# Conv stream of a fused metaformer kernel: two passes of 108 rows with shifts made by four loads a step, in place of three passes of 72 rows and one load

## The reference

```
z = layernorm over channels (x)
z[:, :12] = conv3x3(z[:, :12], w_pc)          # 12 -> 12 channels, zero padding
z = 1x1 conv to 254 channels
z = irfft2( rfft2(8x8 patches of z) * fft_w ) # per channel frequency weights
a, b = halves of z;  x = x + 1x1 conv to 48 ( gelu(a) * b )
t = x as tokens; x = t + FFN( layernorm(t) )  # FFN rounds operands to fp8 (5,2), sums to (5,10)
```

## Time and profile before

| | |
|---|---|
| median of 3 runs | 765.3 us (762.51 to 765.31) |
| profiled execution | 768.14 us, its span 766.3 us, mean granted TensorE clock 0.976 |
| PE busy | 696.4 us (91%) |
| DVE, ACT, POOL busy | 579.6, 550.7, 475.1 us |
| DMA | 62.22 MB, 46492 packets, mean 81 GB/s |
| conv stream on PE (L501) | 384 matmuls, 29.5 us busy |
| taps load (L413) | 32 loads of 292.5 KB |

### The profile page before, as it was taken

One profiled execution on the slowest core, in us unless ns is written; L12 is line 12 of the kernel. 1 busy time (PEld: TensorE's weight loads), 2 busy tenths in 40 slices (PEclk: granted clock), 3 DMA queues, 4 the chain that ended last, 5 costly groups with the idle time before them and its releaser, 6 DMA issues.

```text
span 766.3 us, 18085 instructions
## 1 busy us (share of the span) xinstructions
PE 696.4 (91%) x5547; PEld 507.1 (66%) x5547; DVE 579.6 (76%) x1092; ACT 550.7 (72%) x1090; POOL 475.1 (62%) x356
## 2 busy tenths in 40 slices
PE   1249999999999999999999999999999999999952
PEld 1138777767777777677677776677777777767720
DVE  4614888888888888868888888888888888877651
ACT  3133477778777887767788777878788887766774
POOL 2544666666776676657666766667766776643342
PEclk9998999999999999999999999999999999999985
DMA  3342332333333433234334323333323332231001
GB/s 71 74 91 69 81 73 75 81 99 99 101 74 92 98 98 81 75 93 100 71 94 95 94 67 88 95 100 100 100 66 98 95 98 78 60 98 43 22 21 41
DMA packets 46492, 62.22 MB, mean 81 GB/s; under 512 B 19039, under 2 KB 34871, under 8 KB 46391
## 3 DMA queue, kind: packets, MB, share of 16 engines
q1 hardware_dynamic: 46151, 60.94, 31.9%
q10 hardware_dynamic: 240, 0.05, 0.1%
HBM read 44.62 MB, written 16.35 MB: 80 GB/s over the span
## 4 chain that ended last, share of the span: by engine, by line
PE 73%; DVE 10%; issue 7%; ACT 4%; DMA 2%; POOL 2%; SPq 1%; ACTq 1%; DVEq 0%; POOLq 0%
PE inva L468 15%; PE invb L473 15%; PE mixp L457 12%; PE misc L569 8%; PE misc L528 5%; DVE gmix L845 4%; PE misc L501 4%; PE misc L554 3%; PE misc L627 3%; ACT y L733 3%; PE misc L510 3%; PE misc L482 2%; PE misc L585 2%; DVE st L922 2%; DVE tch L869 1%
## 5 line engine op out<-in xcount | busy, mean ns | idle before, releaser
L845 DVE TENSOR_TENSOR gmix<-mixp,freq_w 128x508 f32<-128x508 f32 x256 | 163.3, 679 | 41.5 <-PE mixp L457 41.5
L457 PE MATMUL mixp<-win,zc 60*128 60x254 f32 x1024 | 145.7, 403 | 6.0 <-DVE gmix L845 2.2
L672 ACT ACTIVATE hid<-misc 128x512 f16<-128x512 f32 x192 | 100.9, 599 | 56.3 <-PE misc L528 56.3
L468 PE MATMUL inva<-inv,gmix 128*127 128x128 f32 x1024 | 136.1, 276 | 1.1 <-DVE gmix L845 1.1
L473 PE MATMUL invb<-inv,gmix 128*127 128x128 f32 x1024 | 135.2, 275 | 0.0
L468 PEld LDWEIGHTS inva<-inv,gmix 128*127 128x127 f32 x1024 | 130.1, 193 | 5.3 <-issue 3.7
L1033 POOL TENSOR_TENSOR tcen<-tpix,st 128x768 f32<-128x768 f32 x32 | 47.2, 1476 | 130.5 <-DVE st L954 130.5
L473 PEld LDWEIGHTS invb<-inv,gmix 128*127 128x127 f32 x1024 | 124.6, 192 | 0.0
L457 PEld LDWEIGHTS mixp<-win,zc 60*128 60x128 f32 x1024 | 88.9, 188 | 50.2 <-issue 27.4
L1015 POOL TENSOR_TENSOR st<-st,neg_half 128x16 f32<-128x16 f32 x32 | 93.8, 2932 | 43.1 <-DVE st L931 43.1
L856 DVE TENSOR_TENSOR hbuf<-gact,invb 127x512 f32<-127x512 f32 x128 | 87.4, 682 | 36.5 <-ACT gact L664 22.6
(11 more groups left out here) (98 smaller groups left out, 1084.7 us busy)
## 6 DMA issues: line engine op xcount, KB each, us to landing
xin<-in_x_dram SPq DMA_DIRECT2D x64, 192.0 KB, 3.4
xres<-in_x_dram SPq DMA_DIRECT2D x64, 192.0 KB, 4.0
out_dram<-ob SPq DMA_DIRECT2D x64, 192.0 KB, 3.5
taps<-cz_scratch SPq DMA_DIRECT2D x32, 292.5 KB
crm<-rm_scratch SPq DMA_DIRECT2D x64, 96.0 KB
cz_scratch<-cz SPq DMA_DIRECT2D x64, 48.8 KB
cx<-in_x_dram SPq DMA_DIRECT2D x32, 96.0 KB
rm_scratch<-rm_t SPq DMA_DIRECT2D x128, 4.0 KB
```

Of the source, the lines that this page charges most:

```text
L457: mm = pe.matmul(mixp[q][:, e * HID2:(e + 1) * HID2], zc[y0:y0 + KC, 2 * s + e, :], win[y0:y0 + KC, :], start=(e == 0), stop=True, skip_gr ...
L468: mm = pe.matmul(inva[0:HID, q * PX:(q + 1) * PX], gmix[:, s % 2, q, 0:HID], inv[:], start=True, stop=True, skip_group_check=True)
L672: act.activation(hid16[:, 3 * c + g, :], bank[banks[g]][:], ACT.Copy).then_inc(hid16_ready, 1)
L845: dve.tensor_tensor(gmix[:, s % 2, 2 * q:2 * q + 2, 0:HID2], mixp[q][:, 0:2 * HID2].rearrange("p (e c) -> p e c", e=2), freq_w[:], ALU.mul ...
```

## The change

The three turns become two. `taps` gets 108 partitions and two buffers, one for each turn. In turn 0 the first 72 partitions hold both parts at the shift dx = 0, in turn 1 at dx = 2; the last 36 partitions hold one part at the middle shift dx = 1: the high part in turn 0, the low part in turn 1. So 3 x 72 = 216 rows of products are covered by 2 x 108. The horizontal shift is now made by the load, since the three blocks of a turn need different ones. The band is therefore loaded by four DMAs: for each turn one of 72 partitions and one of 36, each row 2078 float16 long (4156 bytes, before 4160). All four add to `col_in`, and PE waits for 64 a band in place of 16. A turn has the same four matmuls of 512 columns, out of 108 partitions. The weights are laid out in the same way: `raw_pc`, `pc32` and `wpc` have 108 partitions and 2 turns, filled by six small loads as before.

```diff
-KP = 2 * 3 * CC
+KP = 3 * 3 * CC
+TAPS = SROW * PW - 2
...
-        raw_pc = sb("raw_pc", [KP, 3, CC])
+        raw_pc = sb("raw_pc", [KP, 2, CC])
...
-        pc32 = sb("pc32", [KP, 3, CC])
-        wpc = sb("wpc", [KP, 3, 32], F16)
+        pc32 = sb("pc32", [KP, 2, CC])
+        wpc = sb("wpc", [KP, 2, 32], F16)
...
-        taps = sb("taps", [KP, SROW * PW], F16)
+        taps = sb("taps", [KP, 2, SROW * PW], F16)
...
-                    for part in range(2):
-                        for dx in range(3):
-                            sp.dma_start(raw_pc[part * 3 * CC:(part + 1) * 3 * CC, dx, :],
+                    for turn in range(2):
+                        for block, dx in ((0, 2 * turn), (1, 2 * turn), (2, 1)):
+                            sp.dma_start(raw_pc[block * 3 * CC:(block + 1) * 3 * CC, turn, :],
                                          w_pc[:, :, :, dx].rearrange("o i dy -> (i dy) o")).then_inc(const_in, 16)
...
-                    src = bass.AP(cz_d.tensor, rows16(c) * PW, [[PLANE, 2 * CC], [PW, 3], [1, SROW * PW]])
-                    sp.dma_start(taps[:], src).then_inc(col_in, 16)
+                    for turn in range(2):
+                        both = bass.AP(cz_d.tensor, rows16(c) * PW + 2 * turn, [[PLANE, 2 * CC], [PW, 3], [1, TAPS]])
+                        sp.dma_start(taps[0:6 * CC, turn, 0:TAPS], both).then_inc(col_in, 16)
+                        one = bass.AP(cz_d.tensor, rows16(c) * PW + turn * CC * PLANE + 1,
+                                      [[PLANE, CC], [PW, 3], [1, TAPS]])
+                        sp.dma_start(taps[6 * CC:KP, turn, 0:TAPS], one).then_inc(col_in, 16)
...
-                pe.wait_ge(col_in, upto(16 * (c + 1)))
-                rows = taps[:].rearrange("p (r w) -> p r w", w=PW)
-                for dx in range(3):
+                pe.wait_ge(col_in, upto(64 * (c + 1)))
+                for turn in range(2):
+                    rows = taps[:, turn].rearrange("p (r w) -> p r w", w=PW)
                     for g in range(4):
-                        w0 = 2 * TW * g + dx
-                        src = rows[:, :, w0:w0 + 2 * TW].rearrange("p r (i w) -> p i r w", w=TW)
-                        mm = pe.matmul(bank[2][32 * g:32 * g + 32, :], wpc[:, dx, :], src,
-                                       start=(dx == 0), stop=(dx == 2), skip_group_check=True)
+                        src = rows[:, :, 2 * TW * g:2 * TW * (g + 1)].rearrange("p r (i w) -> p i r w", w=TW)
+                        mm = pe.matmul(bank[2][32 * g:32 * g + 32, :], wpc[:, turn, :], src,
+                                       start=(turn == 0), stop=(turn == 1), skip_group_check=True)
                 mm.then_inc(stream_done, 1)
```

## The result

The changed kernel took 772.1 us (median of 7 runs, 769.11 to 776.08) against 765.31 us (7 runs of before beside it): a ratio of 1.0098, 95% interval 1.0066 to 1.0131, so 5 to 10 us slower. I had forecast 761.4 us, a gain of half a per cent, with a range of 757.5 to 772.5; the time lies inside at its very end, on the other side of no change.

A forecast was written before the change was run, and what follows sets the result against it. PE's own instructions bound the kernel: -6.9 us for the turn, +2.2 at the start, +0.8 in late bands make -3.9, so 764.2 for the profiled execution and 761.4 as median; 8-in-10 range 757.5 to 772.5.

The forecast's parts named there:

- The stream, one turn less: PE's stream: 4 of 12 matmuls go, 0.21 us a step; with 0.4 in the first band, 6.9 us saved.
- Four issues: SyncE's taps loads: 0.90 us per issue, so the fourth starts 2.7 us after the first.
- The time A that PE leaves: From SyncE's issue of a taps load to PE's use: 6.29 to 7.8 us in 29 bands, middle 7.3.
- Landing of the last: Fourth taps load, half the rows, lands 0.5 us sooner: usable 6.45 us after the first issue.
- L: Time from first taps issue to usable taps: 6.45 us, set by the issues, bounds 6.1 and 8.2.
- Start: First band's load, in the chain with nothing over: usable at 6.45 us in place of 4.25, 2.2 lost once.
- Bands in which the load ends too late: Third, fourth and seventh bands: taps late by 0.4, 0.2 and 0.2 us, together 0.8; the other 26 covered.
- The price of a general lateness: Loop of two steps: late taps cost (L - A)/2 - 0.105 us a step; whole saving gone at some L of 7.4.
- Rows that start off: Taps rows in HBM that start 2 or 4 bytes off: costed at nothing.
- The push-back of the output stores and rows_out: SyncE's issues behind the taps loads come 2.7 us later: disappears in its wait for rm_t, 5.7 us each.
- the second: Rival on the taps loads: transfer sets L at some 7.3 us, period falls by only 0.1, 765.3 us; chance 0.18.
- the third: Rival at L495 on PE: the stream waits for taps each step, kernel slower, 770.8 or 778.8 us; chance 0.16.

The follow-up runs named there:

- 144-row kernel: Changed kernel with four issues a band of 36 rows each, 144 rows instead of 216, and two turns of 72 rows: 761.54 us, ratio 0.9948.
- 16-plane: Changed kernel with two loads of 96 rows a band, taken as 16 planes x 6 row offsets, and streams of 96 rows: 760.56 us, ratio 0.9939.
- two-issue kernel: Changed kernel with two issues a band of 108 rows each in place of four, the same bytes: 772.55 us, ratio 1.0099.
- turn-only kernel: Kernel before the change with the middle turn left out, one load of 72 rows as before: 756.92 us, ratio 0.9889.

## Why the prediction was wrong, step by step

- *What bounds the kernel.* Right: PE, and its stream with no cover. One turn less alone gave 8.5 us.
- *The stream, one turn less.* Right in kind, a little too small: 0.25 us a step, my upper bound, in place of 0.21.
- *Four issues.* Nearly right. The fourth starts 3.04 us after the first in the loop, 2.5 outside it, against my 2.7.
- *The time A that PE leaves.* Read right but for the range: of the 29 bands the fifteenth has 9.17 us (336.15 to 345.32, at the loop's seam) and the twenty-fifth 7.88. It changes nothing in the sum.
- *Landing of the last.* This is the step that failed. I took the last load to land 0.5 us sooner than a load by itself, since it has half the rows, and so L = 6.45 us with the issues as what sets it. The row shows 4.34 us from issue to landing in the loop, 4.94 in the first band, in place of 3.6. That it stands behind the rows of the other three fits the 144-row kernel, whose fourth load, with the same 36 rows, lands 3.24 us after its issue in the first band. The bound that I had for this, 898 KB at 233 GB/s and usable at 6.1, used the best quarter of one load for the whole of four. The 16-plane and the 144-row kernels show that the rows for each engine count in the loop; the two-issue kernel shows that in a quiet queue four DMAs are slower than two with the same bytes. How much of the 7.4 us in the loop is rows and how much the number of DMAs stays open, since that kernel also moved the output stores.
- *Start.* Mis-sized by the same L: 7.6 - 4.25 = 3.3 us, for 2.2.
- *Bands in which the load ends too late.* I had 0.8 us in three bands. PE waited in twelve bands after the first, 9.9 us in all. The loop took 1.7 us more, and without waits it would have taken 28 x 0.25 = 7.0 less: 8.7 us (8.9 by PE's waits in it, 10.5 against the turn-only kernel). The forecast had 0.8 for this, and nearly the whole miss of 7.9 us between -3.9 and +4.0 is here, the start's 1.1 being offset by the larger saving. That the terms meet so closely is in part luck, with 2 us open at the loop's seam.
- *The price of a general lateness.* The loop of two steps is there: with one exception a step without a wait follows each that waits. But it hangs by rm_t through HBM (22.06 us from the transpose ahead of one stream to the next stream), not by DVE's work after mix(2). My formula gives -0.05 us a step at L = 7.4; measured is +0.06. Where the other 0.1 us comes from is not shown. A and L both spread from band to band, and I used the middle of each though each late band costs and no early one pays back: the stream at 325.36 alone waited 2.37 us, 9.4 us after the first issue of its taps.
- *Rows that start off.* Right, nothing.
- *The push-back of the output stores and rows_out.* Right: SyncE still waits for rm_t, 92.9 us in 30 times.
- *The rule of the Trainium skill.* The fit in "DMA: Bandwidth & Descriptors", section "Anatomy of one DMA — SWDGE (gpsimd) path", gave 5.9 us from first issue to landing; measured are 7.4, in the loop and in the first band. For four DMAs in a row on this queue the trace does not agree. That DMAs in flight together pay the fixed part side by side was my own step, and not that section's. The page's section "Why a DMA increments its semaphore by 16 and not by 1" bears on it too: the count of engines is the largest up to 16 that divides the outermost size on both sides, 12 here. The shares of 0.72 and 1.07 agree.
- *The rivals.* It lay between the second and the third. The kernel got slower by waits at L495's successor, as the third has it, to which I gave 0.16; but they came in 13 of 32 steps and not in each, at a smaller L than I priced it for. The rate was near that of the second (by the packets 898 KB at some 170 GB/s in the later bands), which I priced at no change. The range of 757.5 to 772.5 took in the measured 772.1 only by the width left for the third.

## What to carry to other kernels

When a cut on the bounding engine is paid for with a larger transfer, find the time by which the transfer must land and size it by rows for each engine, behind all the rows issued with it, and not by one load's best stretch; spare time of 2.6 us for a load of 4.1 is not spare time for three more. Ask which part of a late load depends on the last event: here two thirds of the rows did not, and loading them earlier turned 1% lost into 0.6% gained. An issue that is put ahead of others on a queue delays all behind it, so extra ones belong where the queue waits anyway.

## What the runs showed of the hardware

- The count in the outermost dimension of a load set how many engines shared it: over the first band's two loads share 0.91 at 219 GB/s with 16 planes (1.07 at the peak), 0.72 at 179 with 12, and 9.6 us of kernel time.
- The same 216 rows went at 241 GB/s in two DMAs and at 166 in four, in a queue with nearly nothing else.
- With inverse right behind the stream in place of mix, its first half took 1.08 us for 0.89 and the transposes behind it 0.44 for 0.59; a step of the loop got 0.19 us longer.
- Two loads of 216 rows in all had their last packet 5.3 to 5.6 us after the first issue with no stores beside them, and 7.3 (median) with two output stores issued 2 us behind the first load.
